# Softmax attention with value products in two parts, a pairwise maximum, and more of the shifting on VectorE

## The reference, cut to what matters

```python
q = _qdq(x) @ _qdq(wq).T + bq
kv = cond @ wkv.T + bkv
k, v = jnp.split(kv, 2, axis=-1)
attn = jax.nn.softmax(jnp.einsum('bnhd,bmhd->bhnm', q, k) * scale, axis=-1)
o = jnp.einsum('bhnm,bmhd->bnhd', attn, v).reshape(B, N, C)
out = _qdq(o) @ _qdq(wp).T + bp
```

## Time and profile before

| | us |
|---|---|
| median of 3 runs | 2720.78 |
| lowest and highest run | 2718.15, 2728.79 |
| the profiled execution, its own time | 2719.58 |
| its span, first to last instruction | 2717.7 |
| first score product of softmax attention | 1156.1 |
| its first value product | 1197.7 |
| its last value product | 2413.1 |

### The profile page before, as it was taken

The page is one execution under the profiler, slowest core; times in us unless marked ns, Lnnn a source line. Parts: engine busy times, 40 slices in busy tenths (PEclk is TensorE's granted clock), DMA queues, the critical chain, the costliest instruction groups (busy, mean ns, idle before and its releaser), DMA issues. The chain is left out here.

```text
span 2717.7 us, 74884 instructions
## 1 busy us (share of the span) xinstructions
PE 2407.2 (89%) x30926; PEld 2080.7 (77%) x30926; DVE 1907.8 (70%) x2467; ACT 1493.9 (55%) x2070; POOL 1771.2 (65%) x1225
## 2 busy tenths in 40 slices
PE   5999999999899999488889888898988888859998
PEld 3999999999865665277778777777877777749998
DVE  4888888888752665657777677677767777745554
ACT  2666666666512444156666566665656666624443
POOL 2888888888614888257767667766766777722222
PEclk9999999999989999789999999999999999969999
DMA  4545454445192444211110111011011101041000
GB/s 113 180 136 157 140 156 136 158 139 156 45 282 76 134 132 137 66 47 48 48 48 25 48 48 47 26 47 48 28 45 47 48 26 47 25 150 38 8 8 14
DMA packets 92036, 224.56 MB, mean 83 GB/s; under 512 B 13589, under 2 KB 61954, under 8 KB 87778
## 3 DMA queue, kind: packets, MB, share of 16 engines
q1 hardware_dynamic: 60480, 193.17, 22.7%
q10 hardware_dynamic: 28082, 19.13, 2.3%
q0 software_dynamic: 3216, 8.29, 1.0%
HBM read 193.23 MB, written 27.33 MB: 81 GB/s over the span
## 5 line engine op out<-in xcount | busy, mean ns | idle before, releaser
L1488 POOL TENSOR_TENSOR a_ring<-a_ring,a_tops 125x1792 f32<-125x1792 f32 x128 | 513.3, 4033 | 286.0 <-ACT a_tops L1545 286.0
L1528 ACT COPY a_ring<-a_s 125x1792 f32<-125x1792 f32 x192 | 318.3, 1658 | 202.2 <-PE a_s L1703 202.2
L435 POOL TENSOR_TENSOR l_rows_lo<-l_raw,l_rows_hi 125x512 fp32r<-125x512 f32 x192 | 273.1, 1422 | 105.7 <-ACT l_rows_hi L470 105.7
L1538 ACT ACTIVATE a_ring<-a_ring 125x1792 f32<-125x1792 f32 x192 | 322.7, 1700 | 1.0 <-POOL a_ring L1488 1.0
L438 POOL TENSOR_TENSOR l_phik_lo<-l_phif,l_phik_hi 125x512 fp32r<-125x512 f32 x192 | 297.9, 1551 | 11.8 <-ACT l_phik_hi L476 11.8
L534 DVE TENSOR_TENSOR l_ctxT_lo<-l_rawT,l_ctxT_hi 128x500 fp32r<-128x500 f32 x192 | 213.5, 1112 | 95.9 <-ACT l_ctxT_hi L453 95.8
L80 PE MATMUL l_k<-T_Wk_lo,l_ctxT_hi 128*125 128x256 f32 x768 | 224.9, 293 | 36.1 <-DVE l_phif L551 26.3
L1582 DVE TENSOR_TENSOR a_val<-a_a,bv 125x512 f32<-125x512 f32 x192 | 132.1, 688 | 160.8 <-PE a_a L80 160.7
L1733 PE MATMUL a_x<-a_ring,a_val 125*17 125x56 f32 x12288 | 181.7, 218 | 68.3 <-issue 62.9
L1703 PE MATMUL a_s<-a_qbd,a_keyT 32*125 32x112 f32 x6144 | 226.7, 282 | 15.4 <-issue 10.7
L80 PE MATMUL a_a<-T_wv_lo,a_ctxT_hi 128*125 128x256 f32 x768 | 234.2, 305 | 2.5 <-issue 1.7
(11 more groups left out here) (307 smaller groups left out, 6947.2 us busy)
## 6 DMA issues: line engine op xcount, KB each, us to landing
l_rawT<-in_ctxT SPq DMA_DIRECT2D x32, 1500.0 KB, 6.2
a_rawT<-in_ctxT SPq DMA_DIRECT2D x32, 1500.0 KB, 6.2
l_raw<-in_ctx SPq DMA_DIRECT2D x32, 1344.0 KB
e_wall<-in_L_ffn_w_gate_up SPq DMA_DIRECT2D x8, 1024.0 KB, 14.0
W_hi<-e_xn ACTq DMA_DIRECT2D x32, 192.0 KB, 2.3
W_lo<-e_xn ACTq DMA_DIRECT2D x32, 192.0 KB, 3.0
l_raw<-in_ctx SPq DMA_DIRECT2D x32, 156.0 KB
e_xb<-sorted_x SPq DMA_DIRECT2D x35, 129.0 KB, 2.1
```

What stands on the lines that cost most here:

```text
L435: pool.tensor_tensor(rows.lo[:, sl, 0:D], raw[u][:, sl, :], rows.hi[:, sl, 0:D].bitcast(F32), ALU.subtract).then_inc(rows_lo, 1)
L1488: pool.tensor_tensor(now, now, tops[:, :, :].unsqueeze(2).to_broadcast([CH, 4, 4, TT]), ALU.subtract).then_inc(shifted_late, 1)
L1528: act.copy(chunks_flat(scores_of(u, k, g)), s_bank[0:CH, :, 0:TG]).then_inc(s_copied, 1)
L1538: act.activation(now, now, ACT.Exp).then_inc(exp_done, 1)
```

## The change

Five things, all in `softmax_attention`:

1. The values step X is cut in two parts by r, X00, X01, X10, X11, of 48 products each, with a piece of other work between the two. The first part waits for each of the three exponentials only before the chunks that need it. `x_full` now counts to two for each half.
2. The reduction M over the chunks becomes pairwise. J is cut in two instructions of 896 elements: chunks 2 and 3 of `top` with those of `s_bank`, the result back in `s_bank` (PSUM), and then chunks 0 and 1 into `top`. A new step G (`fold`) has two maxima of 448 elements, one of them into `m_bank`, and M is a third `tensor_tensor` of 448 elements in place of the `tensor_reduce`. Each has exactly one operand in SBUF. The next scores wait for `folded` where they waited for `joined`.
3. Group 1 is shifted on DVE too (`SHIFTS = 2`): U00, U01, U10, U11 on DVE, U02 and U12 alone on POOL.
4. The reciprocal `inv` lies in PSUM, in free columns of `x_bank`, and the two products of D read it there.
5. The four tables have another order.

The core of the diff:

```diff
-    "F0' V1 V3 S10 V2 K12 T0 S11 +K00 M0 "
-    "X1' S12 V5 +K01 V4 F1' +S00 +V0 +K10 +S01 "
-    "T1 +K02 M1 X0 +S02 +K11 "
+    "M1' S01 X00' V1 X01' S02 K10 K12 F0' V3 "
+    "V4 S10 T0 +K00 M0 S11 X10' +K01 X11' S12 "
+    "+V5 F1' +K11 +V2 +V0 +S00 T1 +K02 "
 ).split()
 SCALAR_ORDER = (
-    "K11 E10' E11' C10 E12' C11 K12 Z0 +K00 O1' "
-    "C12 E00 +K01 E01 +C00 E02 +C01 Z1 +K02 +K10 "
-    "O0 +C02 "
+    "C12' K11 E01' E02' C00 Z1' C01 K02 E10' O0' "
+    "C02 K10 K12 E11' E12' C10 Z0 C11 +K00 E00 "
+    "O1' +K01 "
 ).split()
 VECTOR_ORDER = (
-    "P0 U1' J0 V1 V3 M0 V2 D0' R0 P1 "
-    "U0 V5 J1 V4 D1' M1 +V0 R1 "
+    "+V5 J1 G1 M1 +V2 R1 D1' +V0 U10 +P0 "
+    "+V1 U11 +J0 +G0 +M0 +V3 +V4 +R0 D0 +U00 "
+    "+P1 +U01 "
 ).split()
 GPSIMD_ORDER = (
-    "C1 U01' U02' C2 Q1 U11' U12' +Q0 +C0 "
+    "U12' Q1 +Q0 +C0 +C1 +C2 U02 "
...
+SHIFTS = 2
...
             def exp(b, u, k, g):
 
                 n = KC * b + k
-                if g == 0:
-                    act.wait_ge(shifted, n + 1)
+                if g < SHIFTS:
+                    act.wait_ge(shifted, SHIFTS * n + g + 1)
                 else:
-                    act.wait_ge(shifted_late, (KG - 1) * n + g)
+                    act.wait_ge(shifted_late, (KG - SHIFTS) * n + g - SHIFTS + 1)
                 now = chunks_flat(scores_of(u, k, g))
...
-                flat = chunks_flat(top[:, :, :, :])
-                dve.tensor_tensor(flat, s_bank[0:CH, :, 0:TG], flat, ALU.max).then_inc(joined, 1)
+                late = s_bank[0:CH, :, 2 * TT:TG]
+                dve.tensor_tensor(late, late, chunks_flat(top[:, :, 2:4, :]), ALU.max).then_inc(joined_late, 1)
+                early = chunks_flat(top[:, :, 0:2, :])
+                dve.tensor_tensor(early, s_bank[0:CH, :, 0:2 * TT], early, ALU.max).then_inc(joined, 1)
+
+            def fold(b, k):
+
+                n = KC * b + k
+                dve.wait_ge(joined_late, n + 1)
+                dve.wait_ge(joined, n + 1)
+                wait(dve, shifted, SHIFTS * n)
+                wait(dve, tops_kept, n)
+                dve.tensor_tensor(m_bank[0:CH, 0:TG].rearrange("p (j n) -> p j n", j=4), s_bank[0:CH, :, 3 * TT:TG], top[:, :, 1, :], ALU.max).then_inc(folded, 1)
+                dve.tensor_tensor(top[:, :, 0, :], s_bank[0:CH, :, 2 * TT:3 * TT], top[:, :, 0, :], ALU.max).then_inc(folded, 1)
 
             def maximum(b, k):
 
                 n = KC * b + k
-                dve.wait_ge(joined, n + 1)
+                dve.wait_ge(folded, 2 * (n + 1))
                 wait(dve, t_full, n)
-                dve.tensor_reduce(most[:, :, :], top[:, :, :, :].rearrange("p j c n -> p j n c"), AX.X, ALU.max).then_inc(most_done, 1)
+                dve.tensor_tensor(most[:, :, :], m_bank[0:CH, 0:TG].rearrange("p (j n) -> p j n", j=4), top[:, :, 0, :], ALU.max).then_inc(most_done, 1)
...
-            def shift(b, u, k):
+            def shift(b, u, k, g):
 
                 dve.wait_ge(tops_kept, KC * b + k + 1)
-                now = scores_of(u, k, 0)
+                now = scores_of(u, k, g)
...
-                dve.reciprocal(inv[:, :], x_bank[:, sums_at]).then_inc(inv_done, 1)
+                dve.reciprocal(x_bank[:, inv_at:inv_at + TT], x_bank[:, sums_at]).then_inc(inv_done, 1)
                 dve.wait_ge(inv_done, n + 1)
                 for r, to in enumerate((K["attT"], K["odd"])):
                     at = slice(r * L, (r + 1) * L)
-                    dve.tensor_tensor(to[:, k, bass.ds(b * L, L)], outs[:, at], inv[:, at], ALU.mult).then_inc(out_done, 1)
+                    dve.tensor_tensor(to[:, k, bass.ds(b * L, L)], outs[:, at], x_bank[:, inv_at + r * L:inv_at + (r + 1) * L], ALU.mult).then_inc(out_done, 1)
...
-                    wait(pe, joined, n)
+                    wait(pe, folded, 2 * n)
...
-            def values(b, u, k):
+            def values(b, u, k, r):
 
                 n = KC * b + k
-                pe.wait_ge(exp_done, HALF * (n + 1))
-                wait(pe, out_done, 2 * n)
-                if k == 0:
-                    wait_pieces(b, [f"V{g}" for g in range(NP)])
-                for r in range(2):
-                    for ch in range(NC):
-                        for j in range(4):
-                            mm = pe.matmul(x_bank[j * PW:j * PW + HV, r * L:(r + 1) * L], val[u % 2][:, ch, 8 * k + 2 * j + r, :],
-                                           scores_of(u, k, ch // 4)[:, j, ch % 4, r * L:(r + 1) * L], start=(ch == 0), stop=(ch == NC - 1))
+                if r == 0:
+                    wait(pe, out_done, 2 * n)
+                    if k == 0:
+                        wait_pieces(b, [f"V{g}" for g in range(NP)])
+                for ch in range(NC):
+                    if r == 0 and ch % 4 == 0:
+                        pe.wait_ge(exp_done, HALF * n + ch // 4 + 1)
+                    for j in range(4):
+                        mm = pe.matmul(x_bank[j * PW:j * PW + HV, r * L:(r + 1) * L], val[u % 2][:, ch, 8 * k + 2 * j + r, :],
+                                       scores_of(u, k, ch // 4)[:, j, ch % 4, r * L:(r + 1) * L], start=(ch == 0), stop=(ch == NC - 1))
                 mm.then_inc(x_full, 1)
```

More of the change, by code:

```diff
@@ L1390, in softmax_attention @@
         mx, tops = c.sb("a_mx", [TT, 4]), c.sb("a_tops", [CH, 4, TT])
-        outs, inv = c.sb("a_outs", [P, TT]), c.sb("a_inv", [P, TT])
+        outs = c.sb("a_outs", [P, TT])
         one = c.sb("a_one", [P, 2])
@@ L1402, in softmax_attention @@
         paired, joined, most_done = c.sem("a_paired"), c.sem("a_joined"), c.sem("a_most_done")
+        joined_late, folded = c.sem("a_joined_late"), c.sem("a_folded")
         t_full, mx_done, m_full = c.sem("a_t_full"), c.sem("a_mx_done"), c.sem("a_m_full")
@@ L1408, in softmax_attention @@
         x_cleared = c.sem("a_x_cleared")
-        sums_at = slice(256, 256 + TT)
+        sums_at, inv_at = slice(256, 256 + TT), 256 + TT
         block = ctx.enter_context(nc.Block())
@@ L1543, in keep_tops @@
                 act.wait_ge(m_full, n + 1)
-                wait(act, shifted_late, (KG - 1) * n)
+                wait(act, shifted_late, (KG - SHIFTS) * n)
                 act.copy(tops[:, :, :], m_bank[0:CH, 0:TG].rearrange("p (j n) -> p j n", j=4)).then_inc(tops_kept, 1)
@@ L1549, in keep @@
                 n = KC * b + k
-                act.wait_ge(x_full, n + 1)
+                act.wait_ge(x_full, 2 * (n + 1))
                 wait(act, out_done, 2 * n)
@@ L1580, in value_copy @@
                 wait_piece(dve, a_full, w, b)
+                wait(dve, x_full, 2 * KC * (b - 1))
                 split_heads = lambda t: t.rearrange("p c (h e) -> p c h e", h=H)
@@ L1639, in batch @@
                         join(of, int(w[1]))
+                    elif w[0] == "G":
+                        fold(of, int(w[1]))
                     elif w[0] == "M":
@@ L1644, in batch @@
                     elif w[0] == "U":
-                        shift(of, at, int(w[1]))
+                        shift(of, at, int(w[1]), int(w[2]))
                     elif w[0] == "D":
@@ L1710, in turn_maximum @@
                 pe.wait_ge(most_done, n + 1)
-                wait(pe, shifted, n)
+                wait(pe, shifted, SHIFTS * n)
                 for j in range(4):
@@ L1752, in batch @@
                     elif w[0] == "X":
-                        values(of, at, int(w[1]))
+                        values(of, at, int(w[1]), int(w[2]))
                     elif w[0] == "F":
```

2 lines of the change are left out of this document (1 added, 1 removed).

## The result

| | us |
|---|---|
| median of 4 runs | 2581.95 |
| lowest and highest run | 2581.39, 2593.48 |
| the kernel before, median of 4 runs | 2719.47 |
| ratio to before, 95% interval | 0.9498 (0.9463 to 0.9532) |
| the profiled execution, its own time | 2593.48 |

The changed kernel is 5.0% faster, 137.5 us by the medians. The profiled execution is the slowest of the four: its stages ahead of softmax attention took 13.4 us longer than in the profile before (1156.1 to 1169.5 us), and the change does not touch them. The stage itself, from first score product to last value product, went from 1257.0 to 1119.3 us, 137.7 less, which is as much as the difference of the medians; with one profile of each kernel that closeness is partly chance. From first to last value product it was 1215.4 us and is 1083.2.

A forecast was written before the change was run, and what follows sets the result against it. TensorE was taken to bound the kernel: 31.7 work + 0.2 starts + 1.2 "issue" + 0.6 waits + 0.5 clock + 0.4 other = 34.6 us a batch against 38.5, giving 2593 us; range 2545 to 2658.

The forecast's parts named there:

- TensorE's own work of 31.7 us bounds the period: TensorE in softmax attention: values, keys, scores, value products, T, M and sums at full clock take 31.7 us a batch.
- "Issue" is the program not being there in time, at packets' borders: TensorE's idleness without a semaphore, 3.1 us a batch: short records outrun the program; the next packet takes 3.2 us.
- "Issue" falls from 3.1 to 1.2: TensorE's program stalls, us a batch, once the values are parted; bounds 0.3 and 3.1.
- over all positions that a packet's border may have: Counting for TensorE's stalls with a 3.2 us turn: old order 2.4 us a batch, new 0.6.
- The clock back at 0.5 us: TensorE's time lost at low clock falls to 0.5 us a batch from 1.5, between 0.2 and 1.5.
- Waits of 0.6 us a batch for VectorE: TensorE now and then waits at the third group of scores: 0.6 us a batch, between 0 and 1.6.
- The narrow place: M to the third group of scores: VectorE's chain takes 4.85 us, where TensorE has 5.0 us of work.
- 31.7, 0.2 and 0.4: TensorE's us a batch: 31.7 own work, 0.2 added starts of two parts, 0.4 small starts.
- VectorE's prices: VectorE's instructions: 896 elements take 1.09 us, 448 take 0.62, `attT` 0.22, writes to PSUM the same time.
- rival 3: VectorE's join and fold writing PSUM are slow, four times the time by element: 2800 us; chance 0.06.
- rival 1: Parting the values on TensorE gives nothing, 3.1 us a batch stays in place of 1.2: 2653 us; chance 0.17.

The follow-up runs named there:

- unrolled kernel: The changed kernel with 28 batches in a loop's turn in place of 4, so no jump back between batches 2 and 29: 2507.3 us, ratio 0.9228.
- small loads: The changed kernel with one row of 500 numbers loaded in place of 1.5 MB of context for batches 1 to 31: 2548.9 us, ratio 0.9386.

## Why the prediction was right, and where it was not

The time, 2593 forecast and 2582 measured, lies in the range, and the period was forecast as 34.6 and came out as 34.8. Point by point:

- **TensorE's own work of 31.7 us bounds the period** once waits go: right. The unrolled kernel's batches of 31.5 us are that number.
- **"Issue" is the program not being there in time, at packets' borders**: right. The stalls stand multiples of 256 records apart, borders moved by 64 instructions moved them, small loads took away those in keys and values, and parts put together brought them back into the value products. The 2048 instructions that the Trainium skill gives TensorE ("Runtime: NRT & Kernel Launch", "Instruction fetch mechanics") are not borne out: runs of 384 records stalled. What the same section says of a taken branch, that one to a target outside what is held forces a fetch and a stall, agrees: 3.6 us taken against 0.08 not taken.
- **"Issue" falls from 3.1 to 1.2**: mis-sized, 1.7. The step that failed is the counting "over all positions that a packet's border may have". A loop of four batches has one position for each border, repeated in every turn, and this one was bad by 42 us against the one other that was tried; and the jump back, of which I had no term, puts one more stall in each turn. Where borders do take many positions, in the unrolled kernel, "issue" is 6.9 us in 850, 0.26 a batch, so the counting was too dear there: the 1.2 would have been missed on the other side.
- **The clock back at 0.5 us**: wrong, 1.4 (0.04 of 34.8). The premise, both long kinds of idleness gone, did not hold behind the jump: 0.90 in 1505 to 1540 us. The unrolled run had 1.00.
- **Waits of 0.6 us a batch for VectorE**: wrong to the safe side, 0. The narrow place that I named, the pair ahead of the third scores, held: in 900 us TensorE has no wait for VectorE.
- The last three are 2.3 us in the forecast and 3.1 in the trace. What is left of the 34.8 is 31.7, where I had 31.7, 0.2 and 0.4, 32.3 in all. So an error of 0.8 us and one of 0.6 the other way nearly cancelled; that the total is better than its terms is luck. From first to last value product 132.2 us went, against 128; the stage's head, from first scores to first value product, gave 5.5 more (41.6 to 36.1), of which I had no term.
- **VectorE's prices**: right, 1.09 and 0.62 us, `attT` 0.21 us; rival 3 is dead, as the writes to PSUM took within 18 ns of those to SBUF.
- **What each part is worth.** I had parting at 60 us (rival 1, 2653 us). In the old order it gave 17 us, from the changed kernel 23, without jumps 53. The step that failed is that a stall taken away was subtracted whole: in the changed kernel part of it came back at other steps and behind the jump, and in the old order the new place of the scores let VectorE's chain hold the batch at 36.8 us. The maxima, whose worth I had folded into "waits", give 57 to 62, the largest piece of those undone one by one; the new order by itself was not tried. The shift on VectorE and the reciprocal in PSUM, each undone alone, show none.

## What to carry to other kernels

Where an engine's idle time has no semaphore behind it and falls in the midst of its shortest instructions, look at its instruction stream: spread dense runs out, and test the reading by a few dozen idle instructions ahead of the loop, which is the cheapest experiment of all and here won 1.6% by itself. Before pricing a stall at its full length, ask which period the next chain allows, and whether what you put in its place makes that chain longer; here 36.8 us stood 1.7 us a batch below the old mean, and above the best batches of the old order. And a loop that is turned seven times can be cheaper written out: with TURN = 28 it took 2507 us, the least of all runs here.

## What the chip showed that I had not expected

- A jump back in TensorE's program took 3.6 us against 0.08 not taken. With what came behind it, stall and time at the lower clock, it cost at most 5.3 us with the borders better placed (estimate, from 32 us over six jumps).
- 64 idle instructions ahead of a loop were worth 42 us of 2582.
- Stalls of TensorE without a semaphore stood multiples of 256 of its records apart, 34 distances of 34 in the old kernel without jumps.
- DMA loads of 1.5 MB a batch, which no row of TensorE's waits names, cost 30 us over 31 batches; the instruction packets behind them started later, by 1 to 2 us in the kernel before.
